# A normalization's reciprocal roots made once per chunk of four items instead of once per pair, in a fused conv-attention and token-selection kernel

## What is computed

```
u   = layernorm over w of x                         # eps 1e-6
att = softmax over 16x16 head blocks of (wq u)(wk u)^T * scale
o   = wo (att (wv u)) = M u                         # M: one 128x128 matrix per image
y   = (o - mean_w o) * rsqrt(var_w o + 1e-5) * gamma + beta
x   = x + y
z   = layernorm over w of x                         # eps 1e-5
logits = z gate_w^T + gate_b                        # 64 experts
topv, topi = top 8 tokens of each expert by softmax over the tokens
out = x + scatter_add(expert_mlp(sum_k topv * z[topi]) * topv)
```

## Time and profile before

| | before |
|---|---|
| median of 3 runs | 2157.56 us (2151.57 to 2160.16) |
| the profiled execution | 2155.56 us, span 2153.8 us |
| POOL busy over the span | 1939.2 us, 90% |
| ACT | 1882.0 us, 87% |
| PE | 1873.0 us, 87% |
| DVE | 1822.8 us, 85% |
| from 200 to 1600 us | ACT 98.8%, POOL 97.7%, DVE 94.1%, PE 93.0% busy |

### The profile page before, as it was taken

The page is one execution under the profiler, slowest core; times in us unless marked ns, Lnnn a source line. Parts: engine busy times, 40 slices in busy tenths (PEclk is TensorE's granted clock), DMA queues, the critical chain, the costliest instruction groups (busy, mean ns, idle before and its releaser), DMA issues.

```text
span 2153.8 us, 42420 instructions
## 1 busy us (share of the span) xinstructions
PE 1873.0 (87%) x11917; PEld 1286.6 (60%) x11917; DVE 1822.8 (85%) x4612; ACT 1882.0 (87%) x5020; POOL 1939.2 (90%) x2068
## 2 busy tenths in 40 slices
PE   6999999999999999999999999999999987636991
PEld 6866666666666666666666666666666643213570
DVE  4689999999999898989899999999999899624670
ACT  6899999999999999999999999999999987743420
POOL 5799999999999999999999999999999999961387
PEclk9999999999999999999999999999999998765995
DMA  5498888887888888888788888888788676694963
GB/s 188 157 262 222 228 223 206 226 229 216 218 218 235 224 227 210 224 231 222 215 216 231 229 224 220 212 229 227 213 222 223 178 182 162 165 263 124 282 104 32
DMA packets 111068, 447.92 MB, mean 208 GB/s; under 512 B 10575, under 2 KB 52404, under 8 KB 61684
## 3 DMA queue, kind: packets, MB, share of 16 engines
q1 hardware_dynamic: 81140, 302.61, 42.9%
q0 software_dynamic: 29696, 142.61, 34.2%
HBM read 306.78 MB, written 138.41 MB: 207 GB/s over the span
## 4 chain that ended last, share of the span: by engine, by line
ACT 38%; POOL 21%; issue 17%; PE 16%; DVE 5%; ACTq 1%; DMA 1%; POOLq 0%; SPq 0%; DVEq 0%
ACT U L553 16%; POOL U L430 8%; POOL U L435 7%; ACT zT L516 6%; ACT UT L510 6%; PE G L747 4%; ACT LTS L580 3%; ACT LTS L525 3%; PE T L729 3%; PE O L680 2%; POOL zn L451 2%; POOL out_dram L490 2%; PE T L736 1%; ACT zn L574 1%; POOL U L442 1%
## 5 line engine op out<-in xcount | busy, mean ns | idle before, releaser
L553 ACT ACTIVATE U<-xa,nA,rA 128x128 f32<-128x128 f32 x1948 | 803.7, 483 | 2.1 <-issue 1.3
L747 PEld LDWEIGHTS G<-UT 128*128 128x128 f32 x4096 | 536.8, 192 | 226.5 <-issue 225.3
L430 POOL TENSOR_TENSOR U<-U,bet 128x512 f32<-128x512 f32 x512 | 651.4, 1272 | 2.2
L435 POOL TENSOR_TENSOR U<-U,rO 128x512 f32<-128x512 f32 x512 | 532.2, 1040 | 20.3 <-ACT rO L533 19.3
L747 PE MATMUL G<-UT 128*128 128x128 f32 x4096 | 542.0, 275 | 0.0
L680 PE MATMUL O<-U,MT 128*128 128x512 f32 x1024 | 529.5, 599 | 3.0 <-DVE U L938 3.0
L451 POOL TENSOR_TENSOR zn<-U,rZ 128x512 f32<-128x512 f32 x414 | 446.6, 1079 | 11.0 <-ACT rZ L564 10.3
L936 DVE BATCH_NORM_STATS2 stO<-O 128x6 f32<-128x256 f32 x1024 | 386.8, 423 | 50.2 <-PE O L680 49.5
L729 PE MATMUL T<-ident,U 128*128 128x128 f32 x2048 | 324.3, 281 | 119.1 <-ACT UT L510 108.6
L729 PEld LDWEIGHTS T<-ident,U 128*128 128x128 f32 x2048 | 224.6, 142 | 318.1 <-issue 314.1
L954 DVE BATCH_NORM_STATS2 stA<-xa 128x6 f32<-128x256 f32 x1024 | 386.8, 426 | 31.8 <-DMA xa<-in_x 28.5
(11 more groups left out here) (151 smaller groups left out, 1655.0 us busy)
## 6 DMA issues: line engine op xcount, KB each, us to landing
xa<-in_x SPq DMA_DIRECT2D x128, 1024.0 KB, 6.3
U<-in_x POOLq DMA_DIRECT2D x128, 1024.0 KB, 10.8
out_dram<-U SPq DMA_DIRECT2D x128, 1024.0 KB, 8.6
U<-in_L_ffn_weight SPq DMA_DIRECT2D x112, 256.0 KB
LTS<-in_L_ffn_weight SPq DMA_DIRECT2D x16, 256.0 KB
xa<-out_dram,UT POOLq DMA_INDIRECT x64
out_dram<-U,UT POOLq DMA_INDIRECT x64
zT<-in_L_ffn_weight SPq DMA_DIRECT2D x1, 128.0 KB
```

The costliest lines, as they stand in the source:

```text
L430: gp.tensor_tensor(rows(a, i), rows(a, i), bet_b, ALU.add).then_inc(S["gb"], 1)
L435: gp.tensor_tensor(rows(a, i), rows(a, i), rO[:, i // 2 % 2, i % 2 * TI:(i % 2 + 1) * TI].unsqueeze(2).to_broadcast([P, TI, W]), ALU.mult) ...
L553: last = sc.activation(utile(a, i, j), xa[:, k % XR, h * W:(h + 1) * W], ACT.Identity, scale=rA[:, k % 2, h:h + 1], bias=nA[:, k % 2, h:h ...
L747: last = te.matmul(G[:, 0:P], v, v, start=(i == 0 and j == 0), stop=(i == NI - 1 and j == TI - 1))
```

## The change

`Ln` and `Exp` for `rO` are issued once per chunk, over the 16 columns of four items, in place of once per pair over 8. The buffers of statistics and roots grow to match. The lags of the root, of y and of all that follows y change:

```diff
-L_MY, L_BNO, L_RO, L_Y, L_BETA, L_ACC = 57, 59, 60, 62, 63, 67
-L_BNZ, L_STORE, L_RZ, L_ZN = 71, 71, 75, 76
-L_TRZ, L_ZT, L_LOG, L_LTE = 77, 78, 79, 80
-L_MAX, L_MAXI, L_EXP = 89, 91, 92
-S_CROSS, S_TOP, S_TEXP, S_FIN = 121, 122, 123, 124
+L_MY, L_BNO, L_RO, L_Y, L_BETA, L_ACC = 57, 59, 63, 63, 64, 68
+L_BNZ, L_STORE, L_RZ, L_ZN = 72, 72, 76, 77
+L_TRZ, L_ZT, L_LOG, L_LTE = 78, 79, 80, 81
+L_MAX, L_MAXI, L_EXP = 90, 92, 93
+S_CROSS, S_TOP, S_TEXP, S_FIN = 122, 123, 124, 125
...
-        stO = sb("stO", [P, 2, 2 * TI, 3])
-        sO = sb("sO", [P, 2 * TI]); rO = sb("rO", [P, 2, 2 * TI])
+        stO = sb("stO", [P, 2, TC, 3])
+        sO = sb("sO", [P, TC]); rO = sb("rO", [P, 2, TC])
...
-                        pool.wait_ge(S["o_r"], cnt(a, NI // 2, i // 2 + 1))
+                        pool.wait_ge(S["o_r"], cnt(a, NK, i // IC + 1))
...
-                    if r := pair_of(b, t, L_RO):
-                        a, p = r
-                        act.wait_ge(S["o_bn"], cnt(a, NI, 2 * p + 2))
-                        sc.activation(sO[:, :], stO[:, p % 2, :, 2], ACT.Ln, scale=1.0 / W, bias=EPS_O).then_inc(S["o_ln"], 1)
-                        act.wait_ge(S["o_ln"], cnt(a, NI // 2, p + 1))
-
-                        wait(act, S["y"], cnt(a, NI, 2 * p - 2))
-                        sc.activation(rO[:, p % 2, :], sO[:, :], ACT.Exp, scale=-0.5).then_inc(S["o_r"], 1)
+                    if r := item(b, t, L_RO, IC):
+                        a, k = r
+                        act.wait_ge(S["o_bn"], cnt(a, NI, IC * k + IC))
+                        sc.activation(sO[:, :], stO[:, k % 2, :, 2], ACT.Ln, scale=1.0 / W, bias=EPS_O).then_inc(S["o_ln"], 1)
+                        act.wait_ge(S["o_ln"], cnt(a, NK, k + 1))
+
+                        wait(act, S["y"], cnt(a, NI, IC * (k - 1)))
+                        sc.activation(rO[:, k % 2, :], sO[:, :], ACT.Exp, scale=-0.5).then_inc(S["o_r"], 1)
...
-                        wait(dve, S["o_ln"], cnt(a, NI // 2, i // 2 - 1))
+                        wait(dve, S["o_ln"], cnt(a, NK, i // IC - 1))
```

More of the change, by code:

```diff
@@ L433, in body @@
                         pool.wait_ge(S["scaled"], cnt(a, NI, i + 1))
-                        pool.wait_ge(S["o_r"], cnt(a, NI // 2, i // 2 + 1))
+                        pool.wait_ge(S["o_r"], cnt(a, NK, i // IC + 1))
                         gp.tensor_tensor(rows(a, i), rows(a, i),
-                                         rO[:, i // 2 % 2, i % 2 * TI:(i % 2 + 1) * TI].unsqueeze(2).to_broadcast([P, TI, W]),
+                                         rO[:, i // IC % 2, i % IC * TI:(i % IC + 1) * TI].unsqueeze(2).to_broadcast([P, TI, W]),
                                          ALU.mult).then_inc(S["y"], 1)
@@ L930, in body @@
                         dve.wait_ge(S["my"], cnt(a, NI, i + 1))
-                        wait(dve, S["o_ln"], cnt(a, NI // 2, i // 2 - 1))
+                        wait(dve, S["o_ln"], cnt(a, NK, i // IC - 1))
                         o = i % IC * IW
                         for n in range(TI // 2):
-                            h = i % 2 * TI + 2 * n
-                            last = ve.bn_stats(stO[:, i // 2 % 2, h:h + 2, :].rearrange("p n s -> p (n s)"), pair(O[i % NO], n))
+                            h = i % IC * TI + 2 * n
+                            last = ve.bn_stats(stO[:, i // IC % 2, h:h + 2, :].rearrange("p n s -> p (n s)"), pair(O[i % NO], n))
                         last.then_inc(S["o_bn"], 1)
```

## The result

The changed kernel takes 2232.89 us, the median of 4 runs (2231.15 to 2239.71), against 2157.56 before: ratio 1.0347, 95% interval 1.0322 to 1.0372. It is slower, as forecast, by 75 us, where the sum of the prediction was 43, and so above its range (2162 to 2222). The profiled execution took 2231.52 us, span 2229.8.

What follows compares the result with a forecast made beforehand. ACT was taken to set the pace (112.2 of 113.68 us an image), POOL close behind at 111.05. 2155.56 plus 34.7 for 13 images, 3.3, 1.3 and 3.4 gave 2198.3, as a median 2199 us; range 2162 to 2222.

Steps and rivals of the forecast that it cites:

- The saving: On ACT, one Ln and Exp pair fewer per chunk saves 0.40 us, 3.2 us an image.
- Limits A and B: At POOL's y ACT must lead by 0.32 us; at U, waiting for the previous step's zn, by at most 0.83.
- limit B does not bite: Rival: before U ACT runs ahead and absorbs the big Exp, POOL sets the pace; 2128 us, chance 0.13.
- The stall per burst: POOL stands still before y, in steps 7 modulo 8, for 1.10 us once per big Exp.
- A tie: In the chunk without the big Exp, with zn on ACT: ACT's path 13.25 us against POOL's 13.30.
- The small per-image work: Of ACT's 1.45 us an image, some 0.9 (attention, final weights) lies on the stalling path in steps 5 and 6.
- isn't the limit: DVE, which the trace shows waiting for PE, was taken not to limit the kernel, at no cost.
- Ends: Outside the 13 images: three more big Exps +3.3 us, filling +1.3, the later last accumulation +3.4.
- Signs and slips: Expected in the profile: rO's Ln and Exp 128 times each, y waiting some 55 times, ACT and POOL near 95% busy.
- Much slower by collisions: Rival: transfers collide, one more stall of 1 us per chunk of a pair; 2230 to 2260 us, chance 0.08.

Runs made afterwards that it cites:

- e2: Changed kernel with the chunk's roots at lag 62 instead of 63, one step ahead of the first y: ratio 1.0042 to the kernel before.
- e3: Changed kernel with statistics of the sum, store, zn and all behind at the lags of before; root, y, beta, accumulation stay shifted: ratio 1.0257.
- e6: Changed kernel with the root of z, zn and all behind at the lags of before, so zn two steps ahead of U: ratio 1.0243.
- e9: Changed kernel with the big Exp cut to 64 columns of a constant (output no longer the layer's): ratio 1.0041 to the kernel before.
- e5: Changed kernel with POOL issuing the accumulating transfer ahead of the two nA products: ratio 1.0337.
- e12: Changed kernel with SyncE's order turned round, the store ahead of the load: ratio 1.0379.
- e11: Changed kernel with the once-per-image top-8 merging left at its lags of before (121 to 124), one step ahead of max_index: ratio 1.0864.

## Why the prediction was right in kind and too small

- **The saving.** 0.40 us of ACT a chunk is saved, and not worth anything while POOL and ACT are tied so tightly. Held (e2: once untied, the period without its one stall is 111.15, by the prediction POOL's own 111.05).
- **Limits A and B.** Shown. Lifting either one takes the stalls at 7 and 15 away (e2; e3 and e6), and so does taking the burst away (e9). So the mechanism was right, and what failed is the size of three terms of the sum. The rival "limit B does not bite" is refuted by the 1.68 us in front of `U` and by e3.
- **The stall per burst** was mis-sized: 1.41 measured for 1.10, which is 1.2 us an image. I let `zn` end as POOL's next step opens. Behind the issued transfer it ends 0.25 to 0.3 later, which could be read in the earlier trace rows: 1032.04 + 1.25 is 0.25 behind 1033.04. After the change no small `nA` product follows at once, and the delay is carried on through the chunk (y 1.29, `zn` 1.28, beta 1.51). e5 gave 1.14 without it.
- **"A tie" in the other chunk** was the second mis-sized term: 0.5 us at steps 11 and 19 and 0.2 at 27, 1.2 an image, where I had 0. Of the 22 cases of steps 11 and 19, y is 0.77 to 1.11 late in exactly the 11 in which a `UT` of ACT just before had waited 0.44 to 0.50 for PE's transposes, and 0.01 to 0.23 in the others. A lower PE clock has a part in this wait, last section.
- **The small per-image work** was the third. I had 0.9 for it in all. At 23 y is 2.08 - 1.41 = 0.67 later than behind a plain burst, at 31 2.66 - 1.41 = 1.25, in sum 1.0 more than forecast. At 31 it is VectorE that holds ScalarE, over `NM` and over the product. I had dismissed VectorE ("isn't the limit") because the trace shows it waiting for PE most of the time; once an image it is.
- The three make 3.5 us of stall more an image than my 5.3; POOL's own work is 1.0 less than I took (a `nA` product takes 0.22 behind a stall, for 0.42). 2.4 net a period, times 13, is 31 of the missing 33 us.
- **Ends.** Up to step 64 right; behind step 512, +10.1 for 5.6, not taken apart further.
- **Signs and slips.** `Ln` and `Exp` came to 128 each and the busy shares to 93.4 and 93.5% where I had some 95; y waited 71 times over the whole run for "some 55", since the other chunk's stalls came on top. The last step of the prediction's sum has a slip: 2198.3 and the 2.0 to the median make 2200, not 2199.
- **Much slower by collisions**: refuted for the stores by e12. The DMA share fell from 0.83 to 0.78.

Open: how much of e3's and e6's remaining loss near step 31 is VectorE's merging (in e3 the product took 3.0 to 5.5 us in 7 of the 16 images) and how much their own new waits; and what the changed kernel would take with both chains of step 31 lifted.

## What to carry to other kernels

In a pipeline written as steps, each lag difference is slack between two engines, and it has two sides: moving one stage a step later takes the same step from whoever reuses its buffer. Add up each engine's work between the tightest two waits, not over the period; a burst that a step of slack hides becomes a stall in full when the slack on both sides is under the burst. Where two engines are each over 97% busy, a saving on one is worth at most what the other has left, here 2.6 us an image of the 3.2 saved. Try the edit with the least shift first: the same chunk-wise roots with no lag moved behind them were level with before, and with the merging moved away the kernel was 0.65% faster. And where lifting one suspect changes nothing, look whether a second chain ends at the same time before you clear it.

## What the runs showed of the hardware

**A product of two SBUF tiles on VectorE is held off while GpSimd works without a gap.** Eight elements took 0.81 us (median) before, 3.26 in the changed kernel, 1.02 in e5, where one GpSimd instruction runs into the next by under 0.1 and not by 0.3, and 5.35 in e11. They end 0.02 to 0.04 us behind the end of a GpSimd instruction each time, in the changed kernel and e11 the one after which GpSimd stood still. In the changed kernel:

```profile
1139.19 3.27 DVE L1018 TENSOR_TENSOR sm<-eL,XS 128x8 f32<-128x8 f32 x1
...
1140.93 1.50 POOL L430 TENSOR_TENSOR U<-U,bet 128x512 f32<-128x512 f32 x1
```

1139.19 + 3.27 = 1142.46, and the addition ends at 1142.43. The Trainium skill (SBUF — State Buffer, Summary: rules for kernel authors) says that, where VectorE has two SBUF inputs and the GpSimd operation reads SBUF, the second to issue is blocked until the first finishes. The runs agree that it is blocked and go further: in e11 four more GpSimd instructions begin during the wait.

**GpSimd's instructions end later behind a transfer that it issues**, with starts as far apart as ever: beta 1.26 becomes 1.53, y 1.03 becomes 1.29, until a dependent small product or a wait of GpSimd comes by. Busy time grows (651 to 738 us for the same 512 additions) though no work was added; whoever waits for them is released about 0.25 us later (`U` at 1047.00 above starts 0.08 behind the late end of `zn`).

**PE's clock drops after the stalls.** Timeline of the kernel after, PE, steps 333 to 335:

```profile
1077.09 1.05 PE L747 MATMUL G<-UT 128*128 128x128 f32 x8
1080.21 0.63 PE L729 MATMUL T<-ident,U 128*128 128x128 f32 x4 [2.07 <-ACT UT L510]
...
1083.00 1.73 PE L747 MATMUL G<-UT 128*128 128x128 f32 x8
```

```profile
1082.10:1084.80 2.70, 2.70 (x12) 2.01 (x12) 1.55 (x4) 2.67 (x9) 1.57 (x2) 0.57 0.97 316
```

PE idled 2.07 us for ACT; then the granted clock of the stretch is 0.57 (near the 1.2 GHz level) and the same eight matmuls take 1.73 us for 1.05. The next `UT` waits 0.50 us for PE's transposes, and y of step 339 (19 modulo 32) is 1.10 late. From 200 to 1600 us the mean grant is 0.98, where it was 1.00; in e9, without the bursts, it is 1.00 and these stalls are gone.
